# A mixture-of-experts kernel on one core: second-choice scatters moved later, slot loads issued one at a time, prefix sums behind layer 2

## The reference

```python
n1 = layernorm(x)                                  # per token, over 128
agg = epsilon * n1 + adj @ n1                      # adj: 64x64 per graph
h   = silu(rmsnorm(agg @ W1 + b1) * rms_weight)    # 128 -> 512
x   = x + h @ W2 + b2                              # 512 -> 128

n2 = layernorm(x)
logits = n2 @ Wg + bg                              # 8 experts
top_w, top_i = top_k(logits, 2); top_w = softmax(top_w)
out = x + sum over the two chosen experts e of
      top_w * (gelu(n2 @ W1[e] + b1[e]) @ W2[e] + b2[e])   # 128 -> 512 -> 128
```

## Time and profile before

| | |
|---|---|
| time, median of 3 runs | 565.95 us (565.26 to 566.77) |
| the profiled execution's own time | 568.35 us |
| its span (first to last instruction) | 566.4 us |
| busy: TensorE, its weight loads | 488.4 us (86%), 437.6 us (77%) |
| busy: VectorE, ScalarE, GpSimd | 354.4 us (63%), 262.8 us (46%), 361.7 us (64%) |
| first scatter, last scatter | 69.9 us, 289.2 us |
| first write, last write of first choices | 290.4 us, 425.1 us |
| last add | 561.6 us |

### The profile page before, as it was taken

The page is one execution under the profiler, slowest core; times in us unless marked ns, Lnnn a source line. Parts: engine busy times, 40 slices in busy tenths (PEclk is TensorE's granted clock), DMA queues, the critical chain, the costliest instruction groups (busy, mean ns, idle before and its releaser), DMA issues. The chain is left out here.

```text
span 566.4 us, 14003 instructions
## 1 busy us (share of the span) xinstructions
PE 488.4 (86%) x3693; PEld 437.6 (77%) x3693; DVE 354.4 (63%) x1486; ACT 262.8 (46%) x812; POOL 361.7 (64%) x334
## 2 busy tenths in 40 slices
PE   2589889999899998555718999999999999999993
PEld 1467677777677776455618999999999999999993
DVE  6647777666666766226424666767676767676762
ACT  0214123222222332114305777777777777777771
POOL 2323478887788786663473545454556888888886
PEclk9959789999998998977777999999999999999997
DMA  7971122222222221330122222322223555555531
GB/s 251 367 232 29 28 62 69 73 72 72 64 62 64 65 71 35 78 87 16 37 74 72 78 74 86 98 71 65 73 57 51 70 68 73 68 77 74 70 34 14
DMA packets 54577, 45.01 MB, mean 79 GB/s; under 512 B 9522, under 2 KB 46040, under 8 KB 54503
## 3 DMA queue, kind: packets, MB, share of 16 engines
q1 hardware_dynamic: 36480, 26.11, 16.9%
q0 software_dynamic: 16592, 17.13, 15.4%
q10 hardware_dynamic: 1430, 0.88, 0.6%
HBM read 25.75 MB, written 19.25 MB: 79 GB/s over the span
## 5 line engine op out<-in xcount | busy, mean ns | idle before, releaser
L663 ACT ACTIVATE gelu_t<-ps,block_w 128x128 f32<-128x128 f32 x568 | 163.0, 369 | 44.6 <-PE ps L566 25.4
L566 PE MATMUL ps<-slot_t,block_w 128*128 128x128 f32 x1136 | 154.8, 280 | 19.1 <-issue 13.7
L566 PEld LDWEIGHTS ps<-slot_t,block_w 128*128 128x128 f32 x1136 | 141.7, 196 | 20.6 <-issue 14.4
L376 POOL DMA_INDIRECT dispatched_rows<-payload,row_idx x128 | 127.0, 992 | 42.2 <-issue 35.7
L581 PE MATMUL ps<-experts,gelu_t 128*128 x1136 | 152.4, 278 | 0.5 <-ACT gelu_t L663 0.3
L581 PEld LDWEIGHTS ps<-experts,gelu_t 128*128 128x128 f32 x1136 | 140.1, 194 | 1.2 <-issue 1.1
L411 POOL DMA_INDIRECT out_y<-y_out,slot_rows x71 | 112.9, 1590 | 24.2 <-issue 21.3
L408 POOL DMA_INDIRECT out_y<-y_out,slot_rows x71 | 69.7, 982 | 66.2 <-issue 52.3
L942 DVE TENSOR_TENSOR y_bias<-ps,block_w 128x128 f32<-128x128 f32 x142 | 41.5, 292 | 98.3 <-issue 43.4
L930 DVE COPY block_w<-experts 128x644 f32 x142 | 71.1, 501 | 1.4 <-issue 1.3
L498 PE MATMUL ps<-w2e,hidden 128*128 128x136 f32 x512 | 71.8, 291 | 0.0
(11 more groups left out here) (135 smaller groups left out, 453.5 us busy)
## 6 DMA issues: line engine op xcount, KB each, us to landing
slot_rows<-dispatched_rows SPq DMA_DIRECT2D x142, 66.5 KB
xs<-in_x SPq DMA_DIRECT2D x16, 256.0 KB, 6.9
xs_t<-in_x_t SPq DMA_DIRECT2D x16, 256.0 KB, 7.1
experts<-in_f_w SPq DMA_DIRECT2D x16, 256.0 KB, 5.2
out_y<-y_out,slot_rows POOLq DMA_INDIRECT x142
adj_in<-in_adj_t SPq DMA_DIRECT2D x16, 128.0 KB, 6.3
dispatched_rows<-payload,row_idx POOLq DMA_INDIRECT x128
dispatched_rows<-pad_rows SPq DMA_DIRECT2D x18, 66.5 KB
```

The lines of the kernel that those rows point to most:

```text
L376: pool.indirect_dma_start(rows[k], bass.IndirectOffsetOnAxis(row_idx[:, g, j * TOP_K + k:j * TOP_K + k + 1], 0), payload[:, g * JT + j, 0: ...
L566: mm = pe.matmul(bank((2 * i + c // 2) % FH_BANKS, c % 2 * SLOTS, SLOTS), block_w[:, i % BLOCKS, c * P:(c + 1) * P], slot_t[:, i % 2, :], ...
L663: act.activation(gelu_t[:, i % 2, c, :], ps[:, (2 * i + c // 2) % FH_BANKS, c % 2 * SLOTS:(c % 2 + 1) * SLOTS], ACT.Gelu, bias=block_w[:, ...
```

## The change: what it does

Four edits. (1) A scatter is now named by group, part and choice. In step s GpSimd issues the four first-choice scatters of group s - 2, two on each side of the powers, and behind each pair one second-choice scatter out of an ordered list of 64 (`dispatch_second`): 30 of the 64 in the loop. (2) The other 34 are issued between the writes of tiles 0 to 59, one at most behind each. Early and late semaphores count first choices alone; second choices have their own, `second_dispatched`, for which SP waits ahead of tile 71. (3) The first 16 slot loads each wait for a point further on: `h_done`, `prefix_done` or `l2_done` of groups 13 to 15 for tiles 0 to 5, the normalisation of tile i - 6 for tiles 6 to 15; the 16 pads go one behind each load of tiles 16 to 31. (4) On TensorE the prefix sums of group s - 1 come behind the fourth quarter of layer 2, not ahead of it.

```diff
@@ SP
-            def pad(k):
-                for e in range(E):
-                    g = k * E + e
-                    end = sp.value_load(region_end[0:1, g:g + 1], ...)
-                    sp.dma_start(rows[k][bass.ds(end, SLOTS), :], pad_rows[:]).then_inc(padded, 16)
+            def pad(g):
+                end = sp.value_load(region_end[0:1, g:g + 1], ...)
+                sp.dma_start(rows[g // E][bass.ds(end, SLOTS), :], pad_rows[:]).then_inc(padded, 16)
             sp.wait_ge(early_table_ready, 1)
-            sp.wait_ge(early_dispatched, 16 * JT * TOP_K * EARLY_GROUPS)
+            sp.wait_ge(early_dispatched, 16 * JT * EARLY_GROUPS)
             for i in range(RING):
+                if i < 4:
+                    sp.wait_ge((h_done, h_done, prefix_done, l2_done)[i],
+                               (C * (G - 2) + 1, C * (G - 1), G - 2, G - 1)[i])
+                elif i < 6:
+                    sp.wait_ge(h_done, (C * (G - 1) + 1, C * G)[i - 4])
+                else:
+                    sp.wait_ge(slots_normed, i - 5)
                 load_slots(i)
             sp.wait_ge(ends_ready, 1)
-            pad(0)
             for i in range(RING, EARLY):
                 load_slots(i)
-            pad(1)
+                if i - RING < KE:
+                    pad(i - RING)
             sp.wait_ge(tables_ready, 1)
             sp.wait_ge(padded, 16 * (KE + TOP_K))
-            sp.wait_ge(late_dispatched, 16 * JT * TOP_K * (G - EARLY_GROUPS))
-            for i in range(EARLY, NT):
+            sp.wait_ge(late_dispatched, 16 * JT * (G - EARLY_GROUPS))
+            for i in range(EARLY, TILES):
+                load_slots(i)
+            sp.wait_ge(second_dispatched, 16 * JT * G)
+            for i in range(TILES, NT):
                 load_slots(i)
@@ GpSimd
-            def dispatch(g, tiles):
+            def dispatch(g, j, k):
+                if k == 1:
+                    signal = second_dispatched
+                else:
+                    signal = early_dispatched if g < EARLY_GROUPS else late_dispatched
                 pool.wait_ge(rows_ready, g + 1)
...
+            def dispatch_second(n):
+                if n < G * JT:
+                    dispatch(n // JT, n % JT, 1)
...
                 if live(s - 2):
-                    dispatch(s - 2, (0, 1))
+                    dispatch(s - 2, 0, 0)
+                    dispatch(s - 2, 1, 0)
+                if live(s - 3):
+                    dispatch_second(2 * (s - 3))
                 for g in STATS_AT.get(s, ()):
                     pow_ln1(g)
                 if live(s + 2):
                     pow_rms(s + 2)
                 if live(s - 2):
-                    dispatch(s - 2, (2, 3))
+                    dispatch(s - 2, 2, 0)
+                    dispatch(s - 2, 3, 0)
+                if live(s - 3):
+                    dispatch_second(2 * (s - 3) + 1)
             for i in range(NT):
...
+                write_tile(i)
+                done = 2 * (G - 1)
+                left, until = G * JT - done, TILES - 11
+                if i < until and (i + 1) * left // until > i * left // until:
+                    dispatch_second(done + i * left // until)
@@ TensorE
                     second_layer(s, 2)
+                    residual(s, 3)
+                    second_layer(s, 3).then_inc(l2_done, 1)
                 if live(s - 1):
                     prefix(s - 1)
-                if live(s):
-                    residual(s, 3)
-                    second_layer(s, 3).then_inc(l2_done, 1)
```

More of the change, by code:

```diff
@@ L68, in moe_gnn @@
     AHEAD = 4
-    assert D == P and C == 4 and G > 8 and SLOTS == P
+    assert EARLY >= RING + KE and D == P and C == 4 and G > 8 and SLOTS == P
     with ExitStack() as ctx:
@@ L223, in moe_gnn @@
         late_dispatched = sem("late_dispatched")
+        second_dispatched = sem("second_dispatched")
         table_chain = sem("table_chain")
@@ L307, in _ @@
                 sp.dma_start(rows[k][DUMMY:DUMMY + SLOTS, :], pad_rows[:]).then_inc(padded, 16)
-            def pad(k):
-                for e in range(E):
-                    g = k * E + e
-                    end = sp.value_load(region_end[0:1, g:g + 1], min_val=0, max_val=DUMMY - SLOTS)
-                    sp.dma_start(rows[k][bass.ds(end, SLOTS), :], pad_rows[:]).then_inc(padded, 16)
+            def pad(g):
+                end = sp.value_load(region_end[0:1, g:g + 1], min_val=0, max_val=DUMMY - SLOTS)
+                sp.dma_start(rows[g // E][bass.ds(end, SLOTS), :], pad_rows[:]).then_inc(padded, 16)
             def load_slots(i):
@@ L370, in pow_rms, with write_tile @@
                                    ALU.pow).then_inc(rrms_ready, 1)
-            def dispatch(g, tiles):
-                pool.wait_ge(rows_ready, g + 1)
[L374 to L379, removed]
+            def dispatch(g, j, k):
[3 more added lines that the diff above has]
+                    signal = early_dispatched if g < EARLY_GROUPS else late_dispatched
+                pool.wait_ge(rows_ready, g + 1)
+                pool.indirect_dma_start(
+                    rows[k], bass.IndirectOffsetOnAxis(row_idx[:, g, j * TOP_K + k:j * TOP_K + k + 1], 0),
+                    payload[:, g * JT + j, 0:WID], None).then_inc(signal, 16)
+            def dispatch_second(n):
+                if n < G * JT:
+                    dispatch(n // JT, n % JT, 1)
+            def write_tile(i):
+                r = i % RING
+                pool.wait_ge(y_ready, i + 1)
+                token = bass.IndirectOffsetOnAxis(slot_rows[:, r, TOKEN:TOKEN + 1].bitcast(I32), 0)
+                if i < TILES:
+                    pool.indirect_dma_start(out, token, y_out[:, r, :], None, bounds_check=T - 1,
+                                            oob_is_err=False).then_inc(added[r], 16)
+                else:
+                    pool.indirect_dma_start(out, token, y_out[:, r, :], None, bounds_check=T - 1,
+                                            oob_is_err=False, compute_op=ALU.add).then_inc(added[r], 16)
             for s in range(-4, G + 2):
@@ L396, in _ @@
                 if live(s - 2):
-                    dispatch(s - 2, (2, 3))
+                    dispatch(s - 2, 2, 0)
+                    dispatch(s - 2, 3, 0)
+                if live(s - 3):
+                    dispatch_second(2 * (s - 3) + 1)
             for i in range(NT):
-                r = i % RING
                 if i == TILES:
@@ L404, in _ @@
                         pool.wait_ge(added[q], 16 * len(range(q, TILES, RING)))
[L405 to L408, removed]
-                                            oob_is_err=False).then_inc(added[r], 16)
-                else:
-                    pool.indirect_dma_start(out, token, y_out[:, r, :], None, bounds_check=T - 1,
-                                            oob_is_err=False, compute_op=ALU.add).then_inc(added[r], 16)
+                write_tile(i)
[3 more added lines that the diff above has]
+                    dispatch_second(done + i * left // until)
         @block.tensor
```

## The result

| | before | after |
|---|---|---|
| time, median of 4 runs each, side by side | 566.36 us (565.26 to 567.60) | 602.42 us (600.80 to 603.72) |
| ratio after / before | | 1.0635 [1.0599, 1.0671] |
| span of the profiled execution | 566.4 us | 601.1 us |

What follows compares the result with a forecast made beforehand. GpSimd was taken to set the graph stage's pace, TensorE the expert stage's. Terms -11 - 12 - 13 + 12 = -24 us took the profiled 568.35 to 544.3, a median of 542 us; range 518 to 575.

Steps and rivals of the forecast that it cites:

- Graph stage, -11: Graph groups 3 to 14: six scatters a step and later prefix sums make TensorE the bound, saving 11 us.
- Loads one by one, -12: Dip between the stages: separately issued slot loads remove TensorE stalls, saving 12 us, ends zero and 13.
- The first stall: TensorE's first idle wait in the dip between the stages, 6.29 us, costed as gone.
- Start of the expert stage, -13: Tiles 0 to 11: half of 26.1 us of stalls gone, saving 13 us, ends 5 and 26.
- 34 scatters, +12: Writes of the first 60 tiles: added scatters make a tile 2.1 us, losing 12 us, ends 0 and 35.
- the lower end: Added scatters in the expert stage: 0 us lost if writes start with no more than some 15 us delay.
- the ring: Expert stage: 16 slot places, 30 us of tiles, said to hide a write lag of 6 us in all.
- the dip: Slices 17 to 21, 226 to 297 us, between graph and expert stage, where TensorE's busy share falls.
- The upper end: Added scatters in the expert stage: 1.58 us per GpSimd DMA gives 2.48 us a tile, 35 us lost.
- Rival B: Expert stage to tile 60: GpSimd issues without a break, updates are held, 2.97 us a tile, 595 us; chance 0.17.
- Rival C: Tiles 16 to 31: SP is late with loads and pads, gives back about 24 us, 568 us; chance 0.08.
- The cited rule on the shared port: Scatters moved to the expert stage: VectorE copies lock GpSimd out, up to 0.50 us each, 17 us; not added.

Runs made afterwards that it cites:

- e2_spread: Kernel before with only the scatters moved as in the change; loads, pads and prefix sums as before: 597.80 us, ratio 1.0556.
- e9_again: Kernel after with the prefix sums back ahead of the fourth quarter of layer 2, first kind of chip: 600.99 us, ratio 1.0574.
- e1_all8: Kernel after with all eight scatters of a group back in the graph stage: 559.88 us, ratio 0.9882.
- c1_again: Kernel after with eight scatters in the graph stage, old prefix order, memsets spacing GpSimd's DMAs between the stages, first kind of chip: 560.65 us, ratio 0.9891.
- c2_inter: c1_again with pads in two blocks and group 15's scatters one behind each of the first 8 writes: 559.46 us, ratio 0.9899.
- e5_busy: e1_all8 with a scatter-long GpSimd memset at each of the 34 places between the writes: 566.72 us, ratio 0.9984.
- e9_oldprefix: Same kernel as e9_again, run on the other kind of chip: 534.20 us, ratio 1.0102.
- e8_again: e1_all8 with 34 plain GpSimd DMAs of a scatter's size at the places between the writes: 557.95 us, ratio 0.9902.
- c1_paused: Same kernel as c1_again, run on the other kind of chip: 540.00 us, ratio 1.0205.

## Why the prediction was wrong, step by step

- **Graph stage, -11: near in size (-12.1) in part by luck, half right in cause.** The step was "I count 11 groups at 12.65 or more and take 1.0 us each". Groups went from 12.65 to 12.0 us, and from layer 1 of group 3 to that of group 14 before takes 140.4 us and after 134.9: 5.5 us, half of it. Another 6.4 us were won ahead of group 3 (layer 1 at 76.5 and not 82.9), which was not counted; with the old prefix order it begins at 81.1 (e2_spread) and 83.3 (e9_again), so that part is edit 4. The mean square's late update (0.50 us of wait in place of 1.68) is gone. But behind group 3 the six scatters do it alone: with the old prefix order a group takes 11.45 (e2_spread, e9_again). In the new order VectorE waits for the prefix sums, and TensorE then for agg_r. VectorE's timeline in one group after, and TensorE's:

```profile
145.26 0.16 DVE L751 TENSOR_SCALAR mean_sq<-ps 128x4 f32<-128x4 f32 x1 [0.50 <-PE ps L498]
...
147.88 0.23 DVE L809 TENSOR_TENSOR row_cand<-ps,next_row 128x64 f32<-128x64 f32 x1 [2.45 <-PE ps L542]
```

```profile
141.03 1.10 PE L491 MATMUL ps<-agg,quad 128*128 128x512 f32 x2 [0.46 <-DVE agg_r L757]
```

- **Loads one by one, -12: near in size (-9.5), wrong in cause.** The first stall fell from 6.29 to 2.7 us, and tile 0 is copied at 238.5, where "about 237" had been said. But it is the six scatters that did it, the case that the term had as its lower end ("zero if GpSimd's row of scatters alone does it"). From layer 1 of group 15 to the copy of tile 0, on this kind of chip, the kernels with six scatters a step take 17.7 to 21.3 us, and e2_spread, whose 16 loads go out in one go as before, is among them with 17.9. Those with eight scatters and the loads one by one take 21.8 to 26.2, before 27.9. That the number came near was luck.
- **Start of the expert stage, -13: failed (+1.3).** The step was "I take half of the stalls as gone". The four scatters that left the rows were replaced by scatters between the writes, and six in a row, or eight, are still a row: e1_all8 takes 47.6 us here, e2_spread 45.6. On this kind of chip only the kernels with spaced DMAs shorten it (27.2 in c1_again, 29.3 in c2_inter). GpSimd's row after runs without a break from 257.80 to 276.66, fifteen DMAs, and then the engine waits:

```profile
265.37 1.00 POOL L402 DMA_INDIRECT out_y<-y_out,slot_rows  x1 [0.30 <-issue]
...
280.78 0.99 POOL L402 DMA_INDIRECT out_y<-y_out,slot_rows  x1 [4.12 <-DVE y_out L978]
```

- **34 scatters, +12: failed (+48.3, and +5.6 behind tile 60).** This is the step that turned the sign: "I take 2.1 us a tile, nearer to the lower end because the ring helps". Measured were 2.88. The price of 2.1 us a tile came from GpSimd's own length and the ring, and e5_busy confirms that part (2.00). The observation that the term left out stood in the same text: rows of GpSimd's DMAs make other engines' updates late. It was carried to the dip and not to the place where the change writes new rows. The upper end, "eight in 12.65 us, 1.58 each", took the graph stage as undisturbed density, though its update was late by 1.68 us.
- **Rival B, the one given 0.17, is what happened:** 2.97 us a tile and 595 us were worked out, 2.88 and 602 measured. Its counter-argument, "a stalled TensorE starves GpSimd of writes, and the break comes by itself", is also true (GpSimd's 2.13 us breaks) and doesn't help: the break is made of TensorE's lost time, and the next two writes come together.
- **Rival C** did not set the time on these chips. SP is slow beside GpSimd's rows, but the tiles are slower still; on the others its 2.24 us a pair costs the 2.37 us a tile of e9_oldprefix. "Hidden by the same ring" failed there.
- **The cited rule on the shared port** was not added, and the trace after bears that out in size: the 34 scatters between the writes took 964 ns in the median against 958 for the 88 in the graph stage. Six of the 34 did take 1.15 to 1.31 us, each beside 0.32 to 0.48 us of a VectorE copy, while five others beside as much took 0.96 to 0.98; the six cost 1.6 us together, not 17. The same section of the Trainium skill (SBUF — State Buffer, SBUF: two separate sides) says that DMA and compute cannot slow each other and that TensorE and ScalarE never wait on anyone. Instructions indeed kept their length here, a copy 0.27 us in both; but a tile's copy began 1.42 us after its transposition had ended, ScalarE idle for 0.59 of it. So a rule on ports says nothing of updates. Taken as a forecast of time it led to 521 us.

**What stays open.** Whether the hold needs the indirect form of a GpSimd DMA, or only GpSimd DMAs closer than some distance or a list longer than the tile; the rows of e8_again lean to the indirect ones and their spacing, but no run on a chip that holds parts them. By what path the update is delayed. Why two chips show no hold. One more thing differs between the two kinds: all traces have 14003 to 14073 instructions, but 6062 to 6919 recorded semaphore updates on the first kind and 10880 to 11427 on the other. So it is not shown that the hold belongs to the chip itself and not to how its updates are recorded there. And no version tried beats both kernels on both kinds: the best on the first kind, e1_all8, c1_again and c2_inter, are 1.0 to 1.2% under before; c1_paused, the only one of them run on the second, is 2.0% over it.

## What to carry to other kernels

When a trace shows an update that arrives late beside a dense row of DMAs of one engine, price every new row of that kind with the delay, in particular where a chain through three engines comes back within a tile; the engine's busy share (here 9.48 of 19 us) gives no warning. The test of such a delay is one difference, end of the producer to start of its idle consumer, taken tile by tile: 0.04 us or not. Work moved out of a stage that GpSimd bounds must go to gaps that it fits into, and be costed there by itself first. One scatter a gap was not enough here: the gap between two writes was 0.92 us, and a scatter takes 0.96 and 0.30 more to the next DMA.

## What was not expected of the hardware

- On three chips, rows of indirect DMAs of GpSimd 1.3 to 1.6 us apart came with late semaphore updates between TensorE, ScalarE and VectorE, in rows as short as three (2.0 us late at tile 31), while lone writes every 1.9 us held none, nor did the adds of the second choices (1.59 us long, one per 1.895 us).
- Plain GpSimd DMAs (0.60 us), SP DMAs of the same 66.5 KB and memsets (0.99 us) at the same places held nothing.
- The same kernel takes 563 to 568 us on some chips and 529 to 530 on others, a larger difference than the whole change; a ratio taken on one kind says little of the other.
